# A two-layer transformer block on one core: wide unread matmuls beside the gather, a second head split on VectorE, layer 0's side work on other slots, context halves first on GpSimd

## The reference, cut to what matters

```python
xn = _layernorm(x, axis=-1)
x = x + _L0_attn_ref(xn, ...) + _L0_ffn_ref(xn, ...)     # 32 heads of 64, 8 key heads, window of 64; gate * up, 704 wide
xn = _layernorm(x, axis=-1)
x = x + _L1_attn_ref(xn, ...) + _L1_ffn_ref(xn, ...)     # 16 heads of 16, every key; top 64 of 1024 rows through 1024 wide gelu
```

```python
weights = jnp.einsum('bsd,do->bso', x, W_r).squeeze(-1) + b_r
topk_vals, topk_idx = jax.lax.top_k(weights, K)
xg = jnp.take_along_axis(x, topk_idx[..., None], axis=1)
h = jax.nn.gelu(jnp.einsum('bkd,df->bkf', xg, W1) + b1)
blk = jnp.einsum('bkf,fd->bkd', h, W2) + b2
```

## Time and profile before

| | us |
|---|---|
| median of 3 runs | 1100.4 (1098.69 to 1102.31) |
| the profiled execution | 1101.97 |
| its span, first to last instruction | 1100.2 |
| mean granted clock of TensorE | 0.972 of full |
| busy: TensorE, VectorE, ScalarE, GpSimd | 1022.5, 893.1, 800.4, 699.1 |

### The profile page before, as it was taken

The page is one execution under the profiler, slowest core; times in us unless marked ns, Lnnn a source line. Parts: engine busy times, 40 slices in busy tenths (PEclk is TensorE's granted clock), DMA queues, the critical chain, the costliest instruction groups (busy, mean ns, idle before and its releaser), DMA issues. The chain is left out here.

```text
span 1100.2 us, 27320 instructions
## 1 busy us (share of the span) xinstructions
PE 1022.5 (93%) x8858; PEld 648.5 (59%) x8858; DVE 893.1 (81%) x1932; ACT 800.4 (73%) x2112; POOL 699.1 (64%) x982
## 2 busy tenths in 40 slices
PE   3799999999999999999999997989999999899997
PEld 1577887878878878878878873243333333333333
DVE  5998888888888988898897876659989988777872
ACT  4666677767777776776777762269999999778994
POOL 4787787887887987888887764205556554333230
PEclk9999999999999999999999998579999999999999
DMA  6210001000101101001000002300000000000001
GB/s 224 88 44 24 26 18 27 26 19 23 31 13 25 28 14 30 24 18 30 18 24 14 18 18 55 127 1 7 2 3 2 2 2 2 12 11 11 12 2 39
DMA packets 46240, 30.57 MB, mean 28 GB/s; under 512 B 27988, under 2 KB 44180, under 8 KB 45844
## 3 DMA queue, kind: packets, MB, share of 16 engines
q1 hardware_dynamic: 46100, 28.82, 9.0%
HBM read 18.36 MB, written 4.19 MB: 21 GB/s over the span
## 5 line engine op out<-in xcount | busy, mean ns | idle before, releaser
L1342 DVE TENSOR_REDUCE l_mxv<-l_mx 128x1 f32<-128x1024 f32 x256 | 301.2, 1220 | 54.3 <-PE l_mx L1577 51.9
L1225 ACT ACTIVATE l_prob<-l_sc 128x512 f32<-128x512 f32 x512 | 271.4, 610 | 28.8 <-PE l_sc L1585 28.4
L724 POOL TENSOR_TENSOR t<-t 128x320 f32<-128x320 f32 x128 | 110.4, 863 | 101.9 <-DVE t L594 99.5
L1577 PE MATMUL l_mx<-l_kt,l_qt 48*128 48x512 f16 x512 | 161.1, 397 | 7.2 <-DVE l_mxv L1342 7.1
L715 POOL TENSOR_TENSOR rm<-ss,half_neg 128x5 f32<-128x5 f32 x128 | 158.4, 1237 | 8.2 <-DVE ss L627 8.2
L1585 PE MATMUL l_sc<-l_qt,l_kt 50*128 50x512 f16 x512 | 160.7, 385 | 0.3 <-ACT l_prob L1225 0.3
L1558 PE MATMUL l_acc<-l_prob,qkv_all 128*17 128x256 f32 x2048 | 154.8, 386 | 1.4 <-DVE l_acc L1331 1.4
L1420 POOL TENSOR_SCALAR l_mxs<-l_mxv 128x8 f32<-128x8 f32 x32 | 7.5, 235 | 210.9 <-DVE l_mxv L1342 210.9
L881 PEld LDWEIGHTS pv<-v,probs 128*128 128x128 f32 x1024 | 130.6, 191 | 9.5 <-issue 5.0
L376 ACT ACTIVATE nat<-t 128x256 f16<-128x256 f32 (+1 forms) x256 | 79.2, 361 | 72.1 <-POOL t L742 71.3
L881 PE MATMUL pv<-v,probs 128*128 128x65 f32 x1024 | 130.3, 270 | 0.0
(11 more groups left out here) (238 smaller groups left out, 2480.2 us busy)
## 6 DMA issues: line engine op xcount, KB each, us to landing
v<-v SPq DMA_DIRECT2D x240, 16.2 KB, 1.8
qkv_all<-w_qkv SPq DMA_DIRECT2D x3, 768.0 KB, 9.0
xn_all<-xs SPq DMA_DIRECT2D x16, 128.5 KB, 2.0
xa<-x SPq DMA_DIRECT2D x16, 128.0 KB, 2.3
qkv_all<-w_o SPq DMA_DIRECT2D x4, 512.0 KB, 4.4
xc<-x SPq DMA_DIRECT2D x16, 128.0 KB, 2.3
out<-xc SPq DMA_DIRECT2D x16, 128.0 KB, 1.9
l_wt<-w SPq DMA_DIRECT2D x2, 1024.0 KB, 6.0
```

The source lines that it names most:

```text
L724: pool.tensor_tensor(t1[:, b, :, :], t1[:, b, :, :], t2[:, :, :], ALU.add).then_inc(s_["pool_u"], 1)
L1225: act.activation(prob[:, (y * NI + u) % NPR, h * 512:(h + 1) * 512], sc[:, k % NSC, :], ACT.Exp, scale=D1 ** -0.5).then_inc(s_["act_sc"], 1)
L1342: dve.tensor_reduce(mxv[:, x % 2, u:u + 1], mx[:, MX[k] % 2, :], AX.X, ALU.max).then_inc(s_["dve_mx"], 1)
L1577: ins = pe.matmul(mx[:, MX[kx] % 2, keys], qt[r:r + KS, tile % 4, u * P:(u + 1) * P], kt[r:r + KS, tile % 4, keys], start=True, stop=True)
```

## The change

Layer 0: the xn transposes of all pairs but the first go to slots 9 and 15 of the 16 before (`turned_in`), and everything that hangs on `pair_tile` with them, the statistics one slot closer; `way` of odd tiles starts one slot later; the rotation steps on GpSimd are spread (`turning`), the tables go to slots 4, 5, 12 and 16 (`tables`), the third statistics and `xl1` two slots later except for the last two tiles. Layer 1: ten pairs of wide matmuls with unread results (`KEEP_AT`), item 2's split on VectorE, `ctf` evicted without its 15 unused columns in 32, the loads of b1 and b2 behind those of `before` and `slots`, and `cth` and `ctl` ahead of all else in GpSimd's slot.

```diff
+def turned_in(n):
+    return 2 * n if n < B else n // B * 2 * G - (1 if n % B else 7)
...
-    return (n + 2) * G + 21 - n if n >= NT - 2 else (n + 3) * G + 3
+    return (n + 2) * G + 21 - n if n >= NT - 2 else (n + 3) * G + 3 + (n % 2 if n < NT - 3 else 0)
+def turning(s):
+    for n in range(NT):
+        steps = (4, 4, 4) if n >= NT - 2 else (4, 5, 7) if n % 2 else (4, 6, 8)
+        for r in range(3):
+            if way(n) + steps[r] == s:
+                yield n, r
+TABLE_AT = (4, 5, 12, 16)
...
                 if g == 2 and 0 <= n < NT:
...
+                if g == 4 and 0 <= n < NT:
+
                     wait(sp, s_["pool_rope"], n - 1)
                     sp.dma_start(tabr[:, n % 2, :], pos_table[n // B * P:(n // B + 1) * P, 2 * HD:CT]
...
-                n = pair_tile(s + 3)
+                n = pair_tile(s + 2)
                 if n is not None:
                     dve.wait_ge(xa_ld[n % B], n // B * 16 + 16)
...
-                    norm_stats(st3, mv3, ve3, xs[:, par, 0:D], par, "dve_st3", n)
...
-                if g == 5 and 0 <= n < NT:
+                if 0 <= n < NT and g == (3 if n >= NT - 2 else 5):
+                    norm_stats(st3, mv3, ve3, xs[:, n % 2, 0:D], n % 2, "dve_st3", n)
+                if 0 <= n < NT and g == (5 if n >= NT - 2 else 7):
...
-                    wait(pe, s_["dve_xl"], min(NT, s // G // 2 * 2 + 2))
+                    wait(pe, s_["dve_xl"], sum(turned_in(j) < s for j in range(NT)))
...
+KEEP_AT = ((5, 1),) + GATHER_AT + ((6, 6),)
...
-        ctf = sb("ctf", [P, 2, 2, 4, CGR])
+        ctf = sb("ctf", [P, 2, 2, 4, VW])
...
-            sp.wait_ge(ld_s, 16 * 4)
+            sp.wait_ge(ld_s, 16 * 2)
...
+            split(2)
+            dve.wait_ge(ld_s, 16 * 2)
             dve.wait_ge(s_["mod_dve"], MOD["off"])
...
             for c in range(SLOTS):
+                i = c - SLOT_O - 1
+                if 0 <= i < NI:
+
+                    pool.wait_ge(s_["act_sc"], SC["C", i] + 1)
...
-                if item(c) and c > 0:
+                if item(c) and c not in (0, 2):
...
+            def keep_running_beside(c, u):
+
+                k = 1 + (SC["T", c - 2, 1] if u >= 6 else SC["M", c - LAG_M] if c >= LAG_M and u >= 4 else SC["T", c - 2, 0])
+                pe.wait_ge(s_["act_sc"], k + 1 - NSC)
+                for _ in range(2):
+                    pe.matmul(sc[:, k % NSC, :], idh[:, :], idh[:, :].unsqueeze(1).broadcast_to([P, 4, P]), start=True, stop=True)
```

More of the change, by code:

```diff
@@ L100, in pair_tile @@
 def pair_tile(slot):
-    t, g = divmod(slot, G)
-    return t + g // 2 if g in (0, 2) and t % 2 == 0 and 0 <= t < NT else None
+    return next((n for n in range(NT) if turned_in(n) == slot), None)
+def turned_in(n):
+    return 2 * n if n < B else n // B * 2 * G - (1 if n % B else 7)
 WQ_PARTS = (0, 1, 2, 4, 6, 8)
@@ L121, in way, with tables @@
 def way(n):
-    return (n + 2) * G + 21 - n if n >= NT - 2 else (n + 3) * G + 3
+    return (n + 2) * G + 21 - n if n >= NT - 2 else (n + 3) * G + 3 + (n % 2 if n < NT - 3 else 0)
[6 more added lines that the diff above has]
+TABLE_AT = (4, 5, 12, 16)
+def tables(s):
+    if -6 <= s < -2:
+        return 0, s + 6
+    return next(((i, j) for i in range(1, NI) for j in range(4) if (i - 1) * 2 * G + TABLE_AT[j] == s), (None, None))
 def on_way(s, lag):
@@ L343, in _ @@
                     sp.dma_start(v0[WIN:P, n % B, k, :], v1[0:WIN, n % B, k, :]).then_inc(vnw[k], 16)
-                i = (s + 8) // 16
-                if s % 16 == 8 and i < NI:
+                i = 0 if s == -G else s // 16 + 1
+                if (s == -G or s >= 0 and s % 16 == 2) and i < NI:
                     wait(sp, s_["pool_tcw"], i * 4)
@@ L362, in _ @@
                                  ).then_inc(tabr_ld[n % 2], 16)
-                if g == 4 and 0 <= n < NT:
                     sp.wait_ge(s_["dve_wr"], n + 1)
@@ L747, in _ @@
                     rsqrt(rs1[:, n % 2, :], ve1[:, n % 2, :]).then_inc(s_["pool_rs1"], 1)
-                i, part = divmod(s + 6, 16)
-                if part < 4 and i < NI:
+                i, part = tables(s)
+                if i is not None:
                     if part == 0:
@@ L773, in _ @@
                     rsqrt(rs2[:, n % 2, :], ve2[:, n % 2, :]).then_inc(s_["pool_rs2"], 1)
-                if g == 4 and 0 <= n < NT:
+                if 0 <= n < NT and g == (4 if n >= NT - 2 else 6):
                     pool.wait_ge(s_["dve_st3"], 3 * n + 3)
                     rsqrt(rs3[:, n % 2, :], ve3[:, n % 2, :]).then_inc(s_["pool_rs3"], 1)
-                for r in range(3):
-                    n = on_way(s, 4 if s >= (NT + 1) * G + 2 else 4 + r)
-                    if n is None:
-                        continue
+                for n, r in turning(s):
                     heads = qk1_all[:, n % B, n // B, :].rearrange("p (h d) -> p h d", d=D1)[:, :, 0:ROT1]
@@ L1412, in _ @@
             for c in range(SLOTS):
+                i = c - SLOT_O - 1
+                if 0 <= i < NI:
+                    pool.wait_ge(s_["act_sc"], SC["C", i] + 1)
+                    if i >= 2:
+                        pool.wait_ge(s_["pe_mx"], MX["Y", i - 2] + 1)
+                    pool.tensor_copy(cth[:, i % 2, :, :], ctt[:, i % 2, :, :]).then_inc(s_["pool_ct"], 1)
+                    pool.wait_ge(s_["pool_ct"], 2 * i + 1)
+                    pool.tensor_tensor(ctl[:, i % 2, :, :], ctt[:, i % 2, :, :], cth[:, i % 2, :, :], ALU.subtract
+                                       ).then_inc(s_["pool_ct"], 1)
                 t = c - LAG_M
@@ L1595, in _ @@
                         k = SC["T", t, half]
-                        if t == 0 and half == 0:
-                            pe.wait_ge(s_["dve_split"], 2)
-                        pe.wait_ge(s_["pool_split"], t // 2 * 2 + 1)
+                        if t < 4 and half == 0:
+                            pe.wait_ge(s_["dve_split"], t // 2 * 2 + 2)
+                        pe.wait_ge(s_["pool_split"], t // 2 * 2 + 1 - min(1, t // 2))
                         wait(pe, s_["act_sc"], k + 1 - NSC)
@@ L1666, in _ @@
                 if i == 0:
-                    pe.wait_ge(ld_w, 16 * 4)
+                    pe.wait_ge(ld_w, 16 * 6)
                     pe.wait_ge(s_["dve_ct"], 5)
```

42 lines of the change are left out of this document (18 added, 24 removed).

## The result

The changed kernel takes 1089.15 us (1088.55 to 1090.14 in four executions) where the kernel before took 1100.2 beside it: a ratio of 0.990 (0.988 to 0.992). It is faster, but by 11 us (1%) and not by 31; 1069 was forecast, and 1089.15 lies above the range. The profiled execution took 1088.86 us with a span of 1087.0, 13.1 less than the earlier trace rows.

The account below looks back on a forecast made before the run. TensorE paces layer 0, runs at the lower clock at layer 1's start, and is nearly balanced with ScalarE mid-layer 1. From 1101.97 us, -13 - 7 - 1.5 - 10 = -31.5 gives 1070.5, median 1069; range 1057 to 1087.

Parts of the forecast that it names:

- Context halves: Layer 1, items 26 to 31: cth and ctl first in GpSimd's slot remove TensorE's wait; 10 us less (7 to 11).
- what I named as late next: Items 26 to 31: GpSimd's maxima start 1.1 us later, ending near 931.3, before TensorE's transpose of them near 935.
- Layer 0: Respaced extras shorten seven two-tile periods by 1.9 us each: 13 us less (1 to 25).
- the two named waits: Layer 0, slots 0 to 3: TensorE's waits for qe (1.29 us) and xl (0.61 us), together 1.9 a period.
- between 0 and 0.9: Layer 0, slots 8 to 11: cost in us of 0.9 us more VectorE work from one xn and one xl.
- upper bound of 3.6 a period: Layer 0, slots 0 to 3: at most 3.6 us gained, as VectorE keeps 16.2 us of work there.
- the first pair has none: Layer 0: the first pair lacks the crowded extras in slots 0 to 3, so only seven periods count.
- Eviction: Layer 1: the fold's eviction shrinks from 256 to 136 columns, 0.09 us each, 32 times; 1.5 us less (0 to 3.0).
- Wide matmuls: Start of layer 1: ten pairs bring the clock up through gather and hidden parts; 7 us less (best -12, worst +7).
- rival A: Start of layer 1: the fillers don't lift the clock, +7 instead of -7, giving 1083 us; chance 0.13.
- The price of a pair: Start of layer 1: 0.41 us per wide matmul at the lower clock, 8.2 us for twenty, +7 after waits.
- Split and loads: Start of layer 1: split lies in VectorE's 3.13 us wait, fillers end later than the two loads; nothing gained.

Follow-up runs that it names:

- pair_old: Changed kernel with bridge, layer 0's first layernorm transposes back in slots 0 and 2 of 16, with their statistics, xn and xl: 1086.6 and 1090.1 us.
- rest_old: Changed kernel with bridge, layer 0's rotation steps, tables, third statistics, xl1 and odd tiles' projection start put back, moved transposes kept: 1074.0 and 1076.1 us.
- bridge: Changed kernel plus eight unread wide matmuls ahead of the first pair, where TensorE waits anyway: 1070.7 to 1074.0 us in four executions.
- old_split: Changed kernel with item 2's split back on GpSimd: 1070.1 and 1072.2 us with the clock up, 1088.7 and 1089.0 with it down.
- lift_only: Changed kernel with six wide matmuls at the first of the ten places, one at the others: 1068.9, 1069.4, 1070.9, 1072.1 and once 1085.7 us.
- one: Changed kernel with bridge and one wide matmul instead of two at each of the ten places: 1067.9, 1068.2, 1069.1, 1069.5 and once 1082.4 us.
- six: Changed kernel with six wide matmuls instead of two at each of the ten places: 1079.0 us (1076.9 to 1081.6).
- after_again: The changed kernel itself run once more, nothing altered; its profiled execution kept the clock up in the gather: 1073.2 us.
- fill_only: Kernel before with one edit, the ten pairs of wide matmuls beside the gather: 1092.2 us (1091.0 to 1093.6), ratio 0.991.
- bridge_nofill: Changed kernel with the eight bridging matmuls but without the ten pairs: 1078.7 us (1077.9 to 1080.5).
- no_fill: Changed kernel without its ten pairs of wide matmuls beside the gather: 1080.3 us (1079.5 to 1081.7), ratio 0.981.

## Why the prediction was wrong

**Context halves: right.** Forecast -10 (7 to 11); in the trace -9.1 between the first and the last output product and -1.2 ahead of them, and -11.3 alone. The dip of the clock near 961 went with the wait, as said, and what I named as late next, the maxima, holds up nothing.

**Layer 0: right in sign, a third too large.** The term was 7 x 1.9 = 13. Measured 1.4 a period, and 9.6 at the last projection, 8.8 at the start of layer 1. Slots 0 to 3 became 2.19 us shorter, which looks like the 1.9 of the two named waits and is not: 1.43 of it are waits, 0.76 is TensorE's own work that went elsewhere. What I had put at "between 0 and 0.9" for slots 8 to 11 costs 0.86; I had taken it into the bounds and not into the sum. The upper bound of 3.6 a period could not be reached without less work for TensorE, which stood idle for only 2.41 of the 78.50 us; 1.14 are left after the change. And "the first pair has none" left out the first period, which is 1.1 us longer because of the moved first layernorm. The first projection also starts 0.6 later (14.05 instead of 13.43); pair_old (14.03) and rest_old (14.35) have this too, and its cause stays open. Together 1.7, of which I had kept 1 in the range, for the tables, which are not its cause.

**Eviction: 1.5 forecast, 0 measured.** It is 0.10 us shorter (0.09 forecast), yet the items in the middle stay 10.35 us apart. Half the gain was my guess for an engine as full as TensorE; the row of both at 146 of 150 us left it open, and ScalarE does not set the pace alone. Without pairs the kernel is 21.5 us faster than before, and layer 0 and the halves alone make 21.8: eviction, split and loads together bring nothing that these times can show. They could hide 1.5 us; the pace of the middle could not.

**Wide matmuls: this step failed.** -7 forecast, +9 measured in eight of nine executions: 16 of the 20 us between forecast and result. The step reads: "If they bring the clock up: the same fillers did it from 678 on". Those were four and then twelve in a row, and the clock rose only at 684.3; two a step between narrow work did not lift it in any trace, and a group of six did in the one trace that can show it. I asked whether the pairs lift it, and let them begin at a low clock. The question that decides is whether the clock is still up when they begin, and there my sum had nearly the same end state as the runs: in the ninth execution and with a bridge the gather runs about as forecast (steps of 1.65 us against 1.44, hidden parts 1.1 us each). That the three parts alone add up to 31.4, the 31.5 of the forecast, is luck in part: 10.5, 11.3, 9.6 and nothing for the eviction, against 13, 10, 7 and 1.5. The rival A had the mechanism and a chance of 0.13, which was too low: the rows of before showed the clock falling at 691.2, behind the place of the first pair and ahead of the eight in the gather, and nothing in them showed a thin mix raising it.

**The price of a pair: mis-sized.** 4.86 us for twelve are not all at the lower clock; it rose at 684.3, inside that row. At the lower level one of a pair takes 0.48, not 0.41, so ten pairs last 9.6 us and cost 9, where the bad end of this term was 7.

**Split and loads: nothing in time, not nothing in effect.** Both were costed at zero, and the sum of the parts bears that out. But in the changed kernel the split does not lie in a wait of 3.13 us any more: the rank sums come while it still runs, so that l_pos is 0.7 us late, and TensorE stands 0.89 us ahead of the first spread, where the clock falls in the profiled execution. That this wait is the cause is not shown (old_split fell with 0.37, lift_only stayed up with 0.76). Put back, the loads alone gave four of four executions with the clock up, the split alone two of four, both two of four; so few executions don't tell these apart.

## What to carry to other kernels

In this kernel wide matmuls with unread results held the upper clock more cheaply than they raised it: one of 0.21 us a step held it in four of five executions, and it took a group of six to lift it. So put them into TensorE's waits ahead of the stretch that matters, where they cost nothing, and look in the trace at the clock in the moment when they begin. Count the executions, too: four alike said nothing on the fifth. Where the executions of a kernel fall into two groups, look at each group before the mean.

## What the runs showed of the hardware

- The same kernel takes 1073 or 1088 us, by one fall of the clock at 678 us that comes in some executions and not in others; once down, the clock stayed down for 44 us here.
- Wide matmuls of 512 columns, from the start of a group to the start of what follows: at the lower level 0.54 us for one, 0.96 for two, 2.67 for six (traces of one, the changed kernel and six); at the upper level 0.32, 0.54 and 1.40 (one, after_again, six). The first of a group costs 0.1 us more than the rest.
- TensorE busy 44.00 of 44.30 us stayed at 1.2 GHz when its work is gather, 48-row maxima and two wide matmuls a step; with the same mix it stayed at 2.4 GHz with 26.34 busy of 30.40 where it came in at that level (fill_only).
- Ahead of the gather the clock fell in a wait of TensorE (changed kernel at 677.7, one at 682.7, bridge_nofill at 683.5), in the spread (old_split at 678.5, no_fill at 678.6) and behind the maxima (six at 679.9). What exactly makes the clock fall ahead of the gather in one execution and not in the next stays open.
